# Inverse norms of queries and keys: a logarithm and an exponential on ACT with one Newton step on POOL, in place of a seed and three Newton steps on DVE

## The reference

```python
def l2norm(t):
    return t / jnp.maximum(jnp.linalg.norm(t, axis=-1, keepdims=True), 1e-12)
...
q = l2norm(q) * qs
k = l2norm(k) * ksc
freqs, scale = rotary_tables(n)
...
q = q * cos * scale + rotate_half(q) * sin * scale
```

## Time and profile before

| what | value |
|---|---|
| time, median of 3 runs | 4227.32 us (4221.27 to 4227.56) |
| profiled execution: span from the first to the last instruction | 4218.7 us |
| median of the runs less that span | 8.6 us |
| busy PE, PEld | 4055.8 us (96%), 2950.4 us (70%) |
| busy DVE, ACT, POOL | 3292.4 us (78%), 2422.2 us (57%), 2231.4 us (53%) |
| mean granted TensorE clock | 0.987 |

### The profile page before, as it was taken

The page is one execution under the profiler, slowest core; times in us unless marked ns, Lnnn a source line. Parts: engine busy times, 40 slices in busy tenths (PEclk is TensorE's granted clock), DMA queues, the critical chain, the costliest instruction groups (busy, mean ns, idle before and its releaser), DMA issues.

```text
span 4218.7 us, 144433 instructions
## 1 busy us (share of the span) xinstructions
PE 4055.8 (96%) x63591; PEld 2950.4 (70%) x63591; DVE 3292.4 (78%) x6966; ACT 2422.2 (57%) x4410; POOL 2231.4 (53%) x1352
## 2 busy tenths in 40 slices
PE   5999999887999999999999999999999999999997
PEld 4767777564777777777777777777777777777765
DVE  5345354457888988889888898888888888899995
ACT  3111101244767767667776677677667776776664
POOL 2010010025666666666666666666666666666663
PEclk8999999998999999999999999999999999999999
DMA  4111111001111111111111111111111111111110
GB/s 156 41 61 41 56 46 41 21 2 30 40 37 36 48 49 43 41 36 46 51 43 40 37 46 51 42 37 41 46 46 47 38 41 46 46 47 41 40 38 27
DMA packets 76614, 186.14 MB, mean 44 GB/s; under 512 B 16203, under 2 KB 45014, under 8 KB 71510
## 3 DMA queue, kind: packets, MB, share of 16 engines
q1 hardware_dynamic: 75254, 176.51, 13.6%
q10 hardware_dynamic: 736, 0.40, 0.0%
HBM read 61.25 MB, written 2.36 MB: 15 GB/s over the span
## 4 chain that ended last, share of the span: by engine, by line
PE 67%; DVE 5%; ACT 3%; issue 1%; POOL 1%; DMA 0%; POOLq 0%; DVEq 0%; SPq 0%
PE pQ L1690 15%; PE pTO L1723 9%; PE pS L1674 9%; PE pM L1758 7%; PE pM L1747 7%; PE pTO L1736 7%; PE pC L1792 6%; PE pTO L1704 3%; PE pC L1802 3%; ACT sq L1555 2%; ACT pS L1539 1%; DVE rot L1404 1%; DVE m L1408 1%; DVE n L1419 1%; POOL rot L1322 1%
## 5 line engine op out<-in xcount | busy, mean ns | idle before, releaser
L1322 POOL TENSOR_TENSOR rot<-rot,m 128x1024 f32<-128x1024 f32 x384 | 906.4, 2360 | 385.7 <-DVE m L1408 385.7
L1314 POOL TENSOR_TENSOR rot<-rot,rn 128x1024 f32<-128x1024 f32 x384 | 733.7, 1911 | 280.6 <-DVE rn L102 280.6
L1555 ACT ACTIVATE sq<-pQ 128x1024 f32<-128x1024 f32 x380 | 390.1, 1027 | 437.0 <-PE pQ L1690 436.8
L1331 POOL TENSOR_TENSOR E<-E,rc 128x512 f32<-128x512 f32 x384 | 401.2, 1045 | 346.0 <-DVE rc L1394 345.7
L1723 PEld LDWEIGHTS pTO<-PT,V 64*64 64x64 f32 x24576 | 401.5, 134 | 108.9 <-issue 100.2
L1404 DVE TENSOR_TENSOR rot<-pQ,tabl 128x1024 f32<-128x1024 f32 x380 | 456.9, 1202 | 12.1 <-ACT sq L1555 10.0
L1408 DVE TENSOR_TENSOR m<-pQ,tabl 128x1024 f32<-128x1024 f32 x380 | 461.4, 1214 | 0.0
L1419 DVE TENSOR_REDUCE n<-sq 128x16 f32<-128x1024 f32 x380 | 459.3, 1209 | 0.0
L1674 PEld LDWEIGHTS pS<-kT,qT 64*32 64x32 f32 x24576 | 360.9, 107 | 136.6 <-issue 101.7
L1723 PE MATMUL pTO<-PT,V 64*64 64x32 f32 x24576 | 443.5, 221 | 4.3 <-ACT PT L1564 2.8
L1674 PE MATMUL pS<-kT,qT 64*32 64x64 f32 x24576 | 424.9, 218 | 21.9 <-issue 12.5
(11 more groups left out here) (231 smaller groups left out, 6939.8 us busy)
## 6 DMA issues: line engine op xcount, KB each, us to landing
V<-V SPq DMA_DIRECT2D x192, 384.0 KB, 3.5
b_cB<-b_crow SPq DMA_DIRECT2D x32, 1024.0 KB, 5.9
xs<-XT SPq DMA_DIRECT2D x192, 64.0 KB, 2.9
V<-V SPq DMA_DIRECT2D x96, 128.0 KB, 3.3
ys<-XT SPq DMA_DIRECT2D x192, 64.0 KB, 2.0
wq<-in_wqkv SPq DMA_DIRECT2D x6, 512.0 KB, 4.4
wk<-in_wqkv SPq DMA_DIRECT2D x6, 512.0 KB, 4.2
wv<-in_wqkv SPq DMA_DIRECT2D x6, 512.0 KB, 5.4
```

What stands on the lines that cost most here:

```text
L1314: e.tensor_tensor(r, r, rn[b % 2][:, c:c + HEADS].unsqueeze(2).to_broadcast([P, HEADS, HD]), ALU.mult)\
L1322: e.tensor_tensor(rot[j % RING][:, :], rot[j % RING][:, :], m2[:, :, :].rearrange("p h d -> p (h d)"), ALU.add)\
```

## The change

`roots` is gone from DVE. POOL takes the maximum with 1e-24 and multiplies by -0.5 (`norms_half`, into `rh`), ACT takes the logarithm of the squared norm, scaled by 2 to the 16, and then the exponential of minus half of it with a bias that takes the scaling out again (`norm_log`, `norm_root`, into `rn`), and POOL refines the result by one Newton step of four instructions (`newton`). `unit_scale` now waits for POOL's own last step, and the sums of the keys (`squares`, u = 2), which overwrite `n2`, wait for `norms_half`. On ACT a table set that holds both the logarithm and the exponential is loaded ahead of the loop and, in each pass with a feed-forward part, directly behind the third GELU.

```diff
-        v_nt = Steps(ctx, nc, "dve_nt", f"mn rs*{VRS}")
+        g_h = Steps(ctx, nc, "pool_h", "h")
+        a_rt = Steps(ctx, nc, "act_rt", "ln y")
+        g_nt = Steps(ctx, nc, "pool_nt", "yy hyy hyyc y")
...
                 if u % 2 == 0:
-                    e.wait_ge(v_nt.sem, v_nt.at("rs", b))
+                    e.wait_ge(g_nt.sem, g_nt.at("y", b))
...
+            def norms_half(n):
+                if n is None:
+                    return
+                e.wait_ge(v_red.sem, v_red.at("rd", 4 * n + 1 if n < NP else 4 * n - 1))
+                if n:
+                    e.wait_ge(a_rt.sem, a_rt.at("ln", n - 1))
+                e.tensor_scalar(rh[:, :], n2[:, :], 1e-24, -0.5, ALU.max, ALU.mult).then_inc(g_h.sem, 1)
+
+            def newton(n):
+                if n is None:
+                    return
+                y = rn[n % 2][:, :]
+                e.wait_ge(a_rt.sem, a_rt.at("y", n))
+                e.tensor_tensor(rt[:, :], y, y, ALU.mult).then_inc(g_nt.sem, 1)
+                e.wait_ge(g_nt.sem, g_nt.at("yy", n))
+                e.tensor_tensor(rt[:, :], rt[:, :], rh[:, :], ALU.mult).then_inc(g_nt.sem, 1)
+                e.wait_ge(g_nt.sem, g_nt.at("hyy", n))
+                e.tensor_scalar(rt[:, :], rt[:, :], 1.5, None, ALU.add).then_inc(g_nt.sem, 1)
+                e.wait_ge(g_nt.sem, g_nt.at("hyyc", n))
+                e.tensor_tensor(y, rt[:, :], y, ALU.mult).then_inc(g_nt.sem, 1)
...
                 rotary_add(A, 1)
+                norms_half(K)
+                newton(K)
                 unit_scale(R, 2)
...
                 if u == 2:
-                    e.wait_ge(v_nt.sem, v_nt.at("rs", n))
+                    e.wait_ge(g_h.sem, g_h.at("h", n))
...
-            def roots(n):
-                if n is None:
-                    return
-                e.wait_ge(v_red.sem, v_red.at("rd", 4 * n + 1 if n < NP else 4 * n - 1))
-                e.tensor_scalar(n2[:, :], n2[:, :], 1e-24, None, ALU.max).then_inc(v_nt.sem, 1)
-                vector_rsqrt(e, v_nt, n, "rs", rn[n % 2][:, :], n2[:, :], rh[:, :], rt[:, :])
...
                 squares(A, 1)
-                roots(A if A is not None else NP if R == NP - 1 else None)
                 last_stats(F)
...
+            def norm_log(n):
+                if n is None:
+                    return
+                e.wait_ge(g_h.sem, g_h.at("h", n))
+                e.activation(rl[:, :], rh[:, :], ACT.Ln, scale=-2.0 ** (LIFT + 1)).then_inc(a_rt.sem, 1)
+
+            def norm_root(n):
+                if n is None:
+                    return
+                e.wait_ge(a_rt.sem, a_rt.at("ln", n))
+                e.activation(rn[n % 2][:, :], rl[:, :], ACT.Exp, bias=unlift[:, 0:1], scale=-0.5).then_inc(a_rt.sem, 1)
...
             masked(0, 0)
+            e.preload_act_table_set("natural_log_exp_and_others")
             for A, R, B, Dn, C, F in passes():
+                K = A if A is not None else NP if R == NP - 1 else None
...
                 exponent(B, 1)
+                norm_log(K)
+                norm_root(K)
                 gelu(C, 0)
...
                 gelu(C, 2)
+                if C is not None:
+                    e.preload_act_table_set("natural_log_exp_and_others")
                 masked(B, 3)
```

More of the change, by code:

```diff
@@ L42 @@
 MAGIC = float(0x5F3759DF)
+LN2 = float(np.log(2.0))
 class Steps:
@@ L1143, in transformer_phase @@
     RING = 5
+    LIFT = 16
     with ctx:
@@ L1156, in transformer_phase @@
         rh = sb("rh", [P, 4 * HEADS])
+        rl = sb("rl", [P, 4 * HEADS])
         rt = sb("rt", [P, 4 * HEADS])
+        unlift = sb("unlift", [P, 1])
         m2 = sb("m2", [P, HEADS, HD])
@@ L1226, in transformer_phase @@
         v_f = Steps(ctx, nc, "dve_f", "add bn*2 ag*2 ve out*2")
-        GSET = 2 + 3 + 2 + 2 * 2
+        GSET = 3 + 3 + 2 + 2 * 2
         block = ctx.enter_context(nc.Block())
@@ L1297, in _ @@
             e.memset(n2[:, :], 1.0).then_inc(g_set, 1)
+            e.memset(unlift[:, :], 0.5 * LIFT * LN2).then_inc(g_set, 1)
             for x in xs + ys:
```

## The result

The changed kernel took 4329.35 us (median of 4 runs, 4326.65 to 4332.58) against 4225.47 us before: the ratio is 1.0251, with a 95% interval of 1.0236 to 1.0265. It is slower by 104 us. The span of the profiled execution went from 4218.7 to 4324.8 us.

What follows compares the result with a forecast made beforehand. PE's fixed-order work plus its stalls was taken as the bound. Stalls of 82 x 1.0 + 11 x 0.37 = 86 us on the 4218.7 span give 4305, plus 8.6 for the runs: 4313 us, range 4268 to 4358.

Steps and rivals of the forecast that it cites:

- The bound: Last phase: PE's work in fixed order plus its stalls sets the end; PE idle only 2.8 us in 500.
- DVE's gift: DVE's inverse-norm chain, 4.13 us a pass, removed; the next maximum starts about 0.2 us earlier, gain taken at nothing.
- The stall: Fourth group of scores: PE waits for ACT's mask copy, ready 2512.37 against weights loaded at 2511.33; 1.04 us, say 1.0.
- POOL's first operation: First new 128x64 operation behind POOL's addition: 0.27 us, between memset and multiplication; range 0.15 to 0.71.
- Logarithm and exponential: New ACT operations on 128x64 ahead of GELU's load: 0.26 us and 0.35 us, lower end 0.20 each.
- The step that gave eleven of the last layer's passes 0.37 us each: Last layer's output work already delays PE there; the new chain needs 10.74 us against 10.37, so 0.37 each.
- the 86 of the sum: Whole loss over 93 passes with new norms and feed-forward: 82 x 1.0 + 11 x 0.37 = 86 us.
- The 8.6 us added for the runs: Median of the runs shown lies 8.6 us above the 4218.7 span; added to 4305 to give 4313 us.
- Newton steps covered: POOL's four Newton steps end at 2507.0 and the scaling by 2508.9, ahead of PE's turning at 2510.31.
- Dear operations on POOL: Rival: POOL's small operations take 0.71 us each, stall 1.44 us a pass, 127 us in all, 4354; chance 0.12.
- DVE's time reaching the next rotations: Rival: freed DVE time makes POOL's addition end earlier; 4227, chance 0.08, or 4210, chance 0.09.
- Switches that cost more: Rival: ACT's table loads cost more in their new places, 2.56 us more a pass, 324 us, 4551; chance 0.03.

## Why the prediction was right

- **The bound.** PE's order plus its stalls set the end: right. PE's matmuls are the same in number, and its wait of 106 us for the mask is the loss.
- **DVE's gift.** "So it starts about 0.2 us earlier and is on PE's schedule again": right in the steady passes, where the distance stayed 32.98 us with DVE's roots cut short. DVE's busy time fell by 343 us and not by nearly 400, since the 4.13 us of the chain include the gaps between its instructions; where the rest of that difference lies was not followed up. "I take the gain at nothing" failed at the ends of the phase, where the passes are not the one that I read: the last layer gave back some 8 us.
- **The stall.** Predicted 1.04 us, measured 1.21. The term that was mis-sized is POOL's first operation: 0.27 taken, 0.44 in the trace. The difference of 0.17 is of the size of the whole error, but other small terms met by luck: the operation began 0.09 after the addition's end, where the sum has nothing, and the hand-overs behind it took 0.02 to 0.05, where the sum has 0.05 to 0.08. Logarithm and exponential (0.26 and 0.35) took exactly what was taken from copies and GELU, and the run of ACT from the GELU pair to the third GELU took the 3.58 of the sum.

```profile
L1338 POOL TENSOR_SCALAR rh<-n 128x64 f32<-128x64 f32 x97 | 42.3, 436 | 8.2
L1349 POOL TENSOR_SCALAR rt<-rt 128x64 f32<-128x64 f32 x97 | 37.1, 382 | 8.5
L1351 POOL TENSOR_TENSOR rn<-rt,rn 128x64 f32<-128x64 f32 x97 | 31.3, 322 | 8.1
L1347 POOL TENSOR_TENSOR rt<-rt,rh 128x64 f32<-128x64 f32 x97 | 31.1, 320 | 7.6
L1345 POOL TENSOR_TENSOR rt<-rn 128x64 f32<-128x64 f32 x97 | 28.5, 293 | 73.3 <-ACT rn L1592 73.3
```

- **The reasoning for that size.** "The first operation has one input, so I take 0.27, between memset and multiplication": the two operations with one tensor input are the slowest of the five, not the fastest. The extrapolation for two inputs, 0.29, was good (0.29 to 0.32).
- **The count.** The first 76 distances grew by 95.5 us in all, the last 19 by 9.1 (630.2 against 621.1), and the first combination came 1.5 later (1046.7 against 1045.2): 106.1, the growth of the span. The step that gave eleven of the last layer's passes 0.37 us each was wrong in its way. PE waits 0.92 us for the mask in them, not 0.37 (1.15 in the others), and DVE's relief takes away a delay of about the same size that PE had there before (0.8 us a pass, against the run with the load put back). The net of the eleven is 0.9 us, where the step had 4.
- **Luck in the time.** The span grew by 106 us, 20 more than the 86 of the sum. The 8.6 us added for the runs came out at 4.6 (4329.35 less 4324.8), which took 4 of that back. Those 8.6 were mostly the spread of the runs: on record, each run's time lies about 2 us above its own span.
- **Newton steps covered:** right, by the run without them. The scaling behind them ended some 0.4 us later than in the sum, still about 1.0 ahead of PE's turning.
- **The rivals.** Dear operations on POOL: they came out between the forecast and this rival for the operation that counts, and the Newton part of it is refuted. DVE's time reaching the next rotations: refuted in the steady passes of the changed kernel, where POOL's addition ends 1.81 us ahead of PE's next scores, as before (2504.50 against 2506.31). Switches that cost more: refuted by the changed kernel's own rows, where both loads take 1.28 us with 0.02 us or less beside them.

The time of 4329 us lies 16 us above the forecast and inside its range; the direction and the place of the new wait were as stated.

## What to carry to other kernels

Ask of each instruction that is put into an in-order queue what stands behind it and who waits for that, also for a table load: 1.28 us a pass that cost nothing behind the turned keys cost 39 us in all ahead of a copy that PE waits for. Slack is spent once: a delay that costs nothing by itself takes the cover away from the next one in the queue, and together they cost more than the sum. And time that is freed on an engine which waits for the bound anyway comes back as waiting, except where the pipeline fills and drains.

## What the runs showed of the hardware

- On POOL a TENSOR_SCALAR of 128x64 with one tensor input takes 0.44 us with two arithmetic steps and 0.38 with one, more than a TENSOR_TENSOR of the same size with two inputs (0.29 to 0.32).
- A table load takes 1.28 us and begins 0.02 us after the activation before it, in the old places and in the new ones; an activation whose input is ready begins 0.02 us or less after it. The Trainium skill (ScalarE: Activation LUTs, What ACT_TABLE_LOAD costs) has a drain of about 1.38 us for each switch; no run here shows one.
- DVE's maximum over 128x64 took 1.33 us where its neighbours of the same size took 0.23; it ended 0.05 us after POOL's addition. In the trace of before this holds in 96 of its 97 passes. In the last one no POOL instruction runs beside it, and it took 0.14 us; there the next TENSOR_SCALAR of DVE (L92, 0.20 in other passes) took 1.08 us and ended 0.05 us after a POOL multiplication. So these operations waited for POOL, and about 1.2 us in each pass of what came off DVE was such a wait. DVE's rotation and its sum of squares (L1408 and L1419, 1.21 us each) took no longer beside POOL's work than without it.
